# Splitting and respreading the feature norm's sums between attention and experts, and moving one scaling from GpSimd to VectorE

## The reference, cut to what matters

```python
def _layernorm(x, axis=-1, eps=1e-05):
    m = jnp.mean(x, axis=axis, keepdims=True)
    v = jnp.var(x, axis=axis, keepdims=True)
    return (x - m) / jnp.sqrt(v + eps)

x = x + tanh(g_xattn) * attention(_layernorm(x), ctx, ctx, wq, wk, wv, wo)   # 16 heads, window 64, rotary
x = x + tanh(g_ffn)   * moe(_layernorm(x), shared, routed, router)           # 2 shared, 16 routed, top 4
```

## Time and profile before

| | |
|---|---|
| median of 3 runs | 533.61 us (533.41 to 534.77) |
| the profiled execution's own time | 534.51 us |
| its span, first to last instruction | 532.7 us |
| mean granted PE clock | 0.983 of full |
| busy share PE / DVE / ACT / POOL | 95% / 71% / 57% / 57% |

### The profile page before, as it was taken

The page is one execution under the profiler, slowest core; times in us unless marked ns, Lnnn a source line. Parts: engine busy times, 40 slices in busy tenths (PEclk is TensorE's granted clock), DMA queues, the critical chain, the costliest instruction groups (busy, mean ns, idle before and its releaser), DMA issues.

```text
span 532.7 us, 11908 instructions
## 1 busy us (share of the span) xinstructions
PE 505.9 (95%) x4218; PEld 412.4 (77%) x4218; DVE 379.6 (71%) x1185; ACT 303.1 (57%) x843; POOL 305.8 (57%) x227
## 2 busy tenths in 40 slices
PE   9998999999999999999699996999989997999997
PEld 5787887888888888888678784778767885788885
DVE  5989776666786657997957869875876486755444
ACT  5595866665856567666366952674345434644442
POOL 4999999999998899989689404300440034000000
PEclk9999999999999999999979998899989999999999
DMA  7492142201330212012021083207300730055001
GB/s 252 119 268 76 53 133 87 55 22 37 83 107 3 76 36 57 21 38 75 22 56 36 4 266 130 80 0 245 114 1 0 233 125 1 2 153 206 0 1 39
DMA packets 23722, 44.11 MB, mean 83 GB/s; under 512 B 3952, under 2 KB 6512, under 8 KB 23664
## 3 DMA queue, kind: packets, MB, share of 16 engines
q1 hardware_dynamic: 23664, 43.36, 26.7%
HBM read 33.77 MB, written 2.24 MB: 68 GB/s over the span
## 4 chain that ended last, share of the span: by engine, by line
PE 51%; issue 21%; DVE 14%; POOL 9%; ACT 2%; DMA 1%; POOLq 0%; SPq 0%; DVEq 0%; ACTq 0%
PE ring L1137 35%; PE psO L1331 4%; PE psS L1300 4%; PE psS L1137 3%; PE psT L1312 3%; DVE arena L864 2%; POOL xn L568 2%; POOL rstd_d L560 2%; DVE four L893 2%; DVE arena L861 1%; POOL prob L502 1%; DVE arena L1036 1%; PE psS L1154 1%; DVE part L891 1%; DVE wl L951 1%
## 5 line engine op out<-in xcount | busy, mean ns | idle before, releaser
L1137 PE MATMUL ring<-xTh,wh 128*128 128x512 f32 x268 | 109.9, 410 | 0.1
L1137 PE MATMUL ring<-xTl,wh 128*128 128x512 f32 x268 | 106.2, 396 | 0.0
L1137 PE MATMUL ring<-xTh,wl 128*128 128x512 f32 x268 | 105.7, 394 | 0.0
L645 ACT ACTIVATE oTh<-prob 128x512 fp32r<-128x512 f32 x64 | 40.4, 631 | 77.3 <-DVE prob L926 47.3
L502 POOL TENSOR_TENSOR prob<-prob,rinv 128x512 f32<-128x512 f32 x62 | 68.3, 1102 | 11.7 <-DVE rinv L1046 11.6
L934 DVE TENSOR_TENSOR oTl<-prob,oTh 128x512 fp32r<-128x512 f32 x64 | 45.1, 705 | 33.0 <-ACT oTh L645 32.3
L568 POOL TENSOR_TENSOR xn<-xn,nmean_d 128x512 f32<-128x512 f32 x8 | 11.1, 1405 | 99.2 <-DVE nmean_d L1000 99.2
L1137 PE MATMUL ring<-oTh,wh 128*128 128x512 f32 x136 | 56.9, 418 | 10.2 <-DVE oTl L1050 7.2
L926 DVE TENSOR_TENSOR prob<-sneg,arena 128x512 f32<-128x512 f32 x64 | 49.2, 769 | 19.8 <-ACT sneg L629 19.8
L1137 PEld LDWEIGHTS ring<-xTh,wh 128*128 128x128 f32 x268 | 51.0, 190 | 12.5 <-issue 0.8
L1137 PEld LDWEIGHTS ring<-xTh,wl 128*128 128x128 f32 x268 | 51.0, 190 | 11.9
(11 more groups left out here) (141 smaller groups left out, 1136.6 us busy)
## 6 DMA issues: line engine op xcount, KB each, us to landing
arena<-gate_scratch SPq DMA_DIRECT2D x64, 256.0 KB, 6.3
raw<-in_e SPq DMA_DIRECT2D x18, 256.0 KB, 2.6
raw<-in_w SPq DMA_DIRECT2D x16, 256.0 KB, 3.5
arena<-arena SPq DMA_DIRECT2D x16, 256.0 KB, 3.1
arena<-arena SPq DMA_DIRECT2D x16, 192.0 KB, 3.4
x<-in_xt SPq DMA_DIRECT2D x4, 512.0 KB, 4.4
out<-x SPq DMA_DIRECT2D x16, 128.0 KB, 4.6
xn<-in_x SPq DMA_DIRECT2D x3, 512.0 KB, 5.7
```

Source lines behind the costliest of these rows:

```text
L645: act.activation(gated_parts(n)[0], src, ACT.Copy).then_inc(f_hi, 1)
L1137: last = pe.matmul(out, a, b, start=start and i == 0 and j == 0, stop=stop and i == n - 1 and j == 2, skip_group_check=check)
```

## The change

Each `over_features` is cut in two. `over_blocks` is the reduce L891 alone (the new jobs `sum_x` and `sum_sq`). `over_quadrants` is the copies and the small reduce, and stays in `mean` and `var`. The halves, and the jobs after them, get new places. For batch 0 alone, POOL's `scale` makes only the power, and a new DVE job `grow` makes the two multiplications, two attention steps later. Four weight pieces move one or more steps earlier. The `xlo` and `xhi` of batch 0 move one step later, and the router's wait for `craw` is adapted to it.

```diff
-WEIGHT_STEPS = {6: 11, 7: 12, 8: 13, 11: 14, 12: 15, 41: 16, 45: 17, 49: 18, 51: 19, 53: 20, 55: 21}
+WEIGHT_STEPS = {6: 11, 7: 12, 8: 13, 11: 14, 12: 15, 41: 16, 45: 17, 48: 18, 49: 19, 51: 20, 53: 21}
...
-            jobs += {44: [("turn", 0)], 46: [("mean", 0)], 47: [("centre", 0)], 51: [("square", 0)], 53: [("var", 0)],
-                     55: [("scale", 0)], 57: [("back", 0)], 58: [("xhi", 0)], 59: [("xlo", 0)]}.get(c, [])
+            jobs += {44: [("turn", 0)], 46: [("sum_x", 0)], 47: [("mean", 0), ("centre", 0)], 51: [("square", 0)],
+                     54: [("sum_sq", 0)], 55: [("var", 0), ("scale", 0)], 57: [("grow", 0)], 58: [("back", 0)], 59: [("xhi", 0)],
+                     60: [("xlo", 0)]}.get(c, [])
...
-            for e, kind in ((2, "turn"), (3, "mean"), (3, "centre"), (4, "square"), (5, "var"), (6, "scale"), (7, "back"),
-                            (8, "xhi"), (9, "xlo"), (10, "r"), (11, "rexp"), (12, "pick_a"), (13, "pick_b"), (14, "gT")):
+            late = 0 if b else 1
+            for e, kind in ((2 * late, "turn"), (1 + 2 * late, "sum_x"), (2 + 2 * late, "mean"), (2 + 2 * late, "centre"),
+                            (3 + 2 * late, "square"), (5 + 2 * late, "sum_sq"), (6 + 2 * late, "var"),
+                            (6 + 2 * late, "scale"), (10 + late, "back"), (11 + late, "xhi"), (11 + late, "r"),
+                            (12 + late, "xlo"), (12 + late, "rexp"), (13 + late, "pick_a"), (14 + late, "pick_b"),
+                            (15 + late, "gT")):
                 after[b * NE + e].append((kind, b + 1))
...
-                after[b * NE + 15] += [("spread", 4 * (b + 1) + quarter) for quarter in range(4)]
+                after[b * NE + 16] += [("spread", 4 * (b + 1) + quarter) for quarter in range(4)]
...
-                    link(pool.tensor_tensor(rstd_d[:, :], vare_d[:, :], mhalf_d[:, :], ALU.pow))
+                    power = pool.tensor_tensor(rstd_d[:, :], vare_d[:, :], mhalf_d[:, :], ALU.pow)
+                    if n == 0:
+                        power.then_inc(f_power, 1)
+                        return
+                    link(power)
...
-                    dve.wait_ge(c_lo, KC + B - 1)
+                    dve.wait_ge(xT_lo, B + 1)
...
-            def over_features(halves):
+            def over_blocks(halves):

                 link(dve.tensor_reduce(part[:, :], halves.rearrange("p k m d -> p m k d"), AX_XY, ALU.add))
+
+            def over_quadrants():
+
                 for a in range(4):
                     last = dve.tensor_copy(four[:, :, a], part[QUAD * a:QUAD * (a + 1), :])
                 link(last)
...
+                elif kind == "grow":
+                    dve.wait_ge(f_power, 1)
+                    for k in range(KC):
+                        half = xn_halves[:, k, :, :]
+                        last = dve.tensor_tensor(half, half, rstd_d[:, :].unsqueeze(2).to_broadcast([P, BLOCKS, QUAD]),
+                                                 ALU.mult)
+                    last.then_inc(f_scaled, 1)
...
-                    if (c, job[0]) == (CLOSING - 2, "xlo"):
-                        invert(CLOSING - 2)
                     do(job)
+                if c == CLOSING - 2:
+                    invert(c)
```

More of the change, by code:

```diff
@@ L190, in build @@
         f_var, f_scaled, f_turned = sem("f_var"), sem("f_scaled"), sem("f_turned")
+        f_power = sem("f_power")
         gate_in = [sem(f"gate_in{i}") for i in range(NR)]
@@ L996, in do @@
                     link(dve.transpose(xn_flat, x[:, n, :, :].rearrange("p k n -> p (k n)")))
+                elif kind == "sum_x":
+                    over_blocks(xn_halves)
                 elif kind == "mean":
-                    over_features(xn_halves)
+                    over_quadrants()
                     for a in range(4):
@@ L1002, in do @@
                     last.then_inc(f_mean, 1)
+                elif kind == "sum_sq":
+                    dve.wait_ge(f_squared, n + 1)
+                    over_blocks(turned(n).rearrange("p k (m d) -> p k m d", m=BLOCKS))
                 elif kind == "var":
-                    dve.wait_ge(f_squared, n + 1)
-                    over_features(turned(n).rearrange("p k (m d) -> p k m d", m=BLOCKS))
+                    over_quadrants()
                     for a in range(4):
```

## The result

The kernel after took 519.43 us (median of 4 runs, 519.06 to 520.25), the kernel before on the same chip 533.51 us (533.27 to 534.77, 4 runs). The ratio is 0.9734, 95% interval 0.9714 to 0.9753: 2.7% faster. The forecast was 522.6 us, with a range of 514 to 530 us.

The account below looks back on a forecast made before the run. PE, busy 95%, was taken as the bound, so gains come only from its waits and clock falls. 534.5 + 1.3 - 4.1 - 4.4 - 3.8 = 523.5 us, as a median 522.6; range 514 to 530 us.

Parts of the forecast that it names:

- `y` of unit 12: Attention: without DVE's `var` in step 53 its wait falls from 5.02 to about 0.3 us; saves 4.7, plus 2.4 of clock fall.
- `mean` in two steps: Attention, step 47: the four copies behind `y` take 1.7 us instead of 3.65; price 0, bounds -2 and +1.
- The pieces in unit 11: Attention, steps 48 and 49: weight pieces 18 and 19 make `y` wait 2.8 instead of 0.79 us; +2.0, a fall +1.6.
- `grow` in 57: Attention: two multiplications on DVE take 3.9 us, blocked by POOL; `y` of unit 13 waits about 3.5: +3.2, a fall +1.6.
- Attention in all: Sum of attention's terms: -7.1 + 2.0 + 1.6 + 3.2 + 1.6 = +1.3 us.
- Batches 2 and 3: Experts: `rest_gated` is never late for PE, least margin 1.5 us; saves 4.4 and 3.8 us.
- Batch 1: Experts: waits of 0.4, 0.8, 1.6, 0.2, 0.7, together 3.7 us, against 2.01 + 2.58 and two falls; saves 4.1 us.
- The rule of 2.8 us in one place: Experts: about 2.8 us of DVE work fit in one place without a wait, and 1.5 us in every place.
- Port free in attention (1): Rival: attention's new work finds the port free, -6.4 instead of +1.3 us: 515 us; chance 0.15.
- Gates late (2): Rival: batch 1's gates, with 1.5 us margin, come 1.3 to 2.8 us late, with a fall: 525 to 527 us; chance 0.1.
- The port sets the experts' waits (3): Rival: the port, not the block, sets them, so they stay; attention pays full blocking in `grow`: 537.3 us; chance 0.06.
- The split does nothing (4): Rival: second halves stay as long as the whole, as copies in steps 47 and 55 serialize: 526.5 us; chance 0.07.

Follow-up runs that it names:

- the cut rotation: Kernel after, with POOL's rotation of q of unit 15 covering only 8 of 512 columns: 517.02 us, ratio 0.9669.
- the kernel with all improvements: Kernel after, with `grow` in step 58, pieces 18 to 21 in 50, 51, 54, 58, and experts' later weight pieces one place later: 516.24 us, ratio 0.9652.
- the blocks whole: Kernel after, with only the split of the norm's sums among the experts undone, in all three batches: 519.10 us, ratio 0.9716.
- `grow` and pieces later: Kernel after, with `grow` in step 58 and attention's weight pieces 18 to 21 in steps 50, 51, 54, 58: 516.50 us, ratio 0.9659.

## Why the prediction was right, step by step

**`y` of unit 12** (-4.7 and -2.4): right. It waits 0.23 us, and there is no fall there. The old fall's size fits roughly: from `y` of unit 12 to that of unit 13, without the wait ahead of the latter, PE takes 20.2 us before and 18.0 after, 2.3 us of difference, though the steps between hold other work too.

**`mean` in two steps** (copies of 1.7 us, price 0): right. They took 1.74 us, and `score_max(48)` starts at 233.06 us, 0.2 later than before.

**The pieces in unit 11** (+2.0, a fall +1.6): the mechanism was right; two sizes were off. Piece 18 took the 2.00 us of a blocked one, but piece 19 1.33 instead of 1.72, so `y` waited 2.25, not 2.8. No fall followed. With the old steps 0.88 us of wait remain, so the move costs 1.4. The move of pieces 20 and 21 was priced at nothing; taking piece 21 out of step 55 gave back 0.8.

**`grow` in 57** (3.9 us, wait of 3.5, a fall): the mechanism was right, a wait for L489 and one for the division, as the cut rotation shows. It took 3.46 us, and the 0.4 us of lateness from `var` was not there, so `y` waited 2.34: +2.05 in place of +3.2. The fall came in the profiled execution.

**One argument in that step failed**: "POOL had time there and DVE had none". POOL had no time either once `var` stands in step 55: with the scaling on POOL the transposes wait 1.43 us for the division behind it, and the whole stretch is no shorter. The price was read off a row of DVE, and its alternative was taken from the kernel before, in which `var` came earlier.

**Attention in all** was +1.3 and came out at -2.3. Of the 3.6 us, 1.7 are the two waits (0.55 + 1.15), 1.6 the second fall that did not come, and the rest rounding and the transposes. Three falls in four such waits was the rule used; the runs show that the wait alone doesn't decide it. That one of the two foretold falls came and the other did not is chance, and it is nearly half of what the forecast missed in attention.

**Batches 2 and 3** (-4.4 and -3.8): right; no wait stands there. **Batch 1** (-4.1, waits 0.4, 0.8, 1.6, 0.2, 0.7): measured 0.29, 0.49, 1.30, 0.49 and 0.75 us, and no fall, -4.5. The last one is the router's wait for `back`, which the walk did not name.

**The rule of 2.8 us in one place** held: a whole block of 2.95 us costs 0.28 us if the list comes to it on time. But of the two causes given for the experts' gain, smaller blocks and one more empty place, nearly all is the distances: 12.7 us in all, 1.3 of them by the split's waits. The rows of batch 2 point to the distance between POOL's stretch and `var`; a run with that distance alone was not made.

**The rivals.** Port free in attention (1): not so, the blocked 2.00 and 3.46 us are there, though the result of 519.4 lies about midway between its 515 and the forecast. Gates late (2): no wait for a gate anywhere. The port sets the experts' waits (3): in batches 2 and 3 DVE's stretched instructions are unchanged (1.54, 1.52) and the waits went. In part it holds for batch 1, where the wait of 1.30 us comes from the row of four stretched instructions. The split does nothing (4): its reason did not come, since the copies in steps 47 and 55 took 1.74 and 1.75 us. Among the experts the split does do little, for another reason: the new distances alone already pay. That the sum for the experts came out within 0.4 us of the forecast is therefore no sign that the split earned it.

## What to carry to other kernels

Before a long block is cut into parts, look at what stands in front of it: a block that fits costs little if the list is on time, and empty places behind the stretch that another engine slows (11.4 us here, with the other new distances) were worth far more than the cut (1.3). When a part is moved from one engine to another, price both homes in the new order and not in the old one. And a step that the bound engine's next input waits for is no place for work, even of 2 us; one step later, where the engine idles, `grow` cost 0.8 us less of waits.

## What the runs showed of the hardware that was not expected

**The same wait is followed by a fall of the clock or not.** The wait of 2.25 to 2.27 us had one in the kernel with attention's edits alone and none in the six other profiles that have it; that of 2.33 or 2.34 us had one in both profiles of the kernel after, and none in the four other kernels with the same wait. The transposes' wait of 1.91 us for the division had one (the window at 288 us above), that of 1.92 us in the kernel with all improvements none. With attention's edits alone the experts' waits of 2.02 and 2.59 us had none, and those of 2.83 and 2.84 had one; in the kernel before it was 2.01, 2.58 and the first 2.83 that had one. It changes from execution to execution of one kernel too: of five with the blocks whole three had a mean granted clock of 1.00 (spans 517.0, 517.0, 517.3 us) and two 0.996 and 0.997 (518.3, 519.0). What decides it the runs don't show. A fall's price by these spans is 1.0 to 2.0 us, and 1.6 by the stretch behind `y` of unit 13. But it is not always paid: `grow` and pieces later has spans of 514.5 and 514.7 us at a granted clock of 1.00 and of 514.6 and 514.6 at 0.996, and the kernel after 517.4 at 0.999 and 517.2 at 0.996.

**A fall is partly paid back** by shorter waits behind it, where DVE is what PE waits for (waits of 1.31 and 1.15 us that are absent where falls were, so that two falls cost 0.2 us).

**Not every POOL instruction blocks DVE.** Beside POOL's power of 3.41 us a `gated` of two SBUF inputs took 0.71 us, beside its centring 1.54, in the kernel after (the timeline of all engines):

```profile
380.19 3.41 POOL L566 TENSOR_TENSOR rstd_d<-vare_d,mhalf_d 128x16 f32<-128x16 f32 x1 [5.30 <-DVE vare_d L1024]
...
380.75 0.71 DVE L939 TENSOR_TENSOR prob<-sneg,arena 128x512 f32<-128x512 f32 x1
```

The reduce L901, with a single input, took 1.20 to 1.22 us wherever it stood, also beside POOL's rotation (L500) in attention (at 225.81 and 263.91 us in the kernel after). The Trainium skill ("SBUF — State Buffer", Who interferes with whom) says that a VectorE instruction with two SBUF inputs contends with a GpSimd instruction that reads SBUF and that a reduce never does. The rows agree on the reduce and on the centring. The power reads SBUF as well and did not hold the `gated` up; its operands are 128x16 against the centring's 128x512, and which of size and operation makes the difference no run here shows.
